# Filler products on TensorE: which planned gaps get them, in which bank, and how many

## The chip, the cores and the metric

The kernel runs on one core of one Trainium2 chip. The metric is device time in microseconds (us) of that core. Engine names are those of the profile: PE is TensorE's matmul, PEld its weight load, DVE is VectorE, ACT is ScalarE, POOL is GpSimd, SP is SyncE, which issues most transfers.

## The reference, cut to what matters

The reference is a chain of eight blocks on an activation `x` of 4 x 512 x 128 floats. Each takes the layer norm of x and adds its result back:

```python
x = x + L0_xcond(cond, ctx, _layernorm(x), ...)  # slot attention, 77 context rows, 3 iterations
x = x + L0_ffn(_layernorm(x), ...)               # routed experts, 8 of 128 -> 512 -> 128, top 2
x = x + L1_xcond(ctx, _layernorm(x), ...)        # attention, 16 heads of 64, over [ctx, x]
x = x + L1_ffn(_layernorm(x), ...)               # routed experts, top 1
x = x + L2_xcond(_layernorm(x), cond, ctx, ...)  # self attention, cross attention, gated ffn
x = x + L2_ffn(_layernorm(x), ...)               # 16 gated experts, top 2, and shared ones
x = x + L3_xcond(_layernorm(x), cond, ctx, ...)  # 6 layers: self and cross attention (16 heads of 8), ffn
x = x + L3_ffn(_layernorm(x), ...)               # router and ffn for half of the rows
```

None of this arithmetic is touched by the change. Filler products compute nothing that is used: `warm` multiplies the identity tile by itself (128 x 128 by 128 x 256, bf16) into a PSUM bank that the next real product overwrites.

## The kernel before

**Tiles and streams.** The four batch items stay in SBUF in `X`. Up to four streams of work run interleaved, in two sets of scratch tiles whose names begin with `c0` and `c1`. All products go to PSUM, which is cut into eight banks of 128 x 512 floats (four pairs). Every matmul in the profile therefore writes `ps`.

**The planner.** The order of work on each engine is fixed while the program is built. Each stream is a Python generator that yields wants: a chain of (engine, cost in us) steps, the buffers that it takes, and the time `after` which its data is ready. `Plan.merge` asks `Plan.ends` for the planned begin and end of each stream's next want, takes the one with the least key (its begin, with small weights), moves the planned clocks of the engines that the chain uses, takes the buffers and resumes the stream, which appends the step to `order` (`emit`). Each engine then walks this one list and issues its part of each step, in that order. Costs in the wants are hand-measured, `SLOW` scales them, `ORDER` holds the constants of each stage. Semaphores make the order safe; the plan's times have no force on the chip.

**Stages.** "0" is the slot attention (`stage0`, wants named `s0...`), "1" and "3" the routed experts (`routed`, products `re1` L1856 and `re2` L1866 behind `zbt` L1847), "2" and "4" the attentions with 64-wide heads (`attn64`: `mt` L1969, `sc` L1982, `av` L1998), "5" the gated experts, "6" the six layers (`attn6`: row maxima `m8` L2137, with DVE L2970 behind it, `m8t` L2159 and `m8w` L2168, scores `s8` L2179, `a8` L2193 and L2110 for the projections), and at the end of each stream `stage7`.

**Wants that matter here.** Most wants that use PE begin with it: `[("T", .6), ("A", .68)]` is a product and its eviction by ACT. Four begin on another engine and take a bank: `s0a` (DVE .35, then PE 1.3; L1755 and L1756, four times), `en` (DVE, POOL, DVE, then PE .2; L1808, once), `m8t` (DVE .42, PE .35; 48 times in stage 6) and `m8w` (DVE .5, PE .35; 24 times). Products that add to a bank which their stream already holds (`av`, `re2`, `a8` after the first) take no bank of their own.

**Filler before.** `Plan.idle` looks only at a want whose chain begins with PE and whose first buffer is a bank. The planned idle time is `w.after` less the later of PE's planned clock and the planned release of its buffers. If it is over 0.7, a `warm` step goes ahead of the want, into the want's own bank, with 0.6 of the idle time divided by 0.107 us products, at most 24. `warm` (L1714 to L1720) waits until the bank is free and issues its products without any other wait, so they start as soon as PE gets to them.

Of the kernel before, what the change touches and what calls it, by code (L numbers as in the profile page):

```python
# [31 lines left out]
    "6": dict(lag=0.0744, weight=0.0116, even=0.002, held=0.2624, table=1.1712, apart=55.6204, spread=0, seed=7961, stagger=13.3148, bias=dict(T=0.244, S=0.373, VTA=-0.191, TVb=-0.054, A=-0.534, VG=-0.949, G=-0.49, TA=-0.046, TAb=-0.043, TAV=0.203), turns=((13, 247, 0.3), (53, 150, 0.0), (379, 276, 0.3), (419, 456, 0.0), (3849, 853, 0), (3874, 138, 0.15), (3874, 642, 1.0), (4746, 100, 0), )),  # L32
}
PER_SEM = 8000
WARM_OVER, WARM_SHARE, WARM_MOST = 0.7, 0.6, 24
S128 = float(np.float32(128.0) ** np.float32(0.5))
S8 = float(np.float32(1.0) / np.float32(np.sqrt(np.float32(8.0))))

# [1 line left out]
class Sem:  # L40


    def __init__(self, nc, ctx, name, by=1):
        self.nc, self.ctx, self.name, self.by = nc, ctx, name, by
        self.n, self.tab, self.handles = 0, {}, []
# [56 lines left out]
class Bufs:  # L102
# [13 lines left out]
    def give(self, u, t=0.0):  # L116
        u.t = t
        self.free.append(u)
# [11 lines left out]
class Banks:  # L130
# [13 lines left out]
    def take(self):  # L144
# [6 lines left out]
        self.held[k] = True  # L151
        return u

    def give(self, u, t=0.0):
        u.t = t
        for k in u.at:
            self.use[k], self.held[k] = u, False
# [54 lines left out]
class Plan:  # L212


    def __init__(self):
        self.order, self.live, self.table = [], [], None
        self.clock = {"T": 0.0, "A": 0.0, "V": 0.0, "G": 0.0, "S": 0.0}

# [46 lines left out]
        self.would = table  # L265
        return (t if begin is None else begin) + self.held * held, r

    def idle(self, w):

        if not w.bufs or not isinstance(w.bufs[0], (Banks, Pairs, Last)):  # L270
            return 0.0
        ready = max(self.clock["T"], max(b.ready(w.bufs.count(b)) for b in w.bufs))
        return w.after - ready

    def merge(self, streams, owners=()):
        for s, o in zip(streams, list(owners) + [None] * len(streams)):
            self.spawn(s, o)
        idle = 0
        while self.live:
            idle += 1  # L280
            if idle > 6:
                raise RuntimeError("the streams wait for each other")
            best = None
            for x in list(self.live):
                if x[1] is None:
                    try:
                        x[1] = x[0].send(x[2])
                    except StopIteration:
                        self.live.remove(x)
                        idle = 0  # L290
                        continue
                    x[2] = None
                if x[1] is None:
                    continue
                e = self.ends(x[1])
                if e is None:
                    continue
                key = e[0] + (self.even * x[3].work if x[3] else 0.0) + self.weight * (e[1][-1][2] if e[1] else 0.0)
                key += self.bias.get(x[1].kind, 0.0)
                if self.spread:  # L300
                    key += self.spread * self.rng.rand()
                if best is None or key < best[0]:
                    best = (key, x, e[1], self.would)
            if best is None:
                continue
            idle = 0
            _, x, ends, self.table = best
            self.steps += 1
            idle_pe = self.idle(x[1]) if x[1].chain and x[1].chain[0][0] == "T" else 0.0
            if self.turns and self.steps >= self.turns[0][0]:  # L310
                _, seed, self.spread = self.turns.pop(0)
                self.rng = np.random.RandomState(seed)
            for eng, t, _ in ends:
                self.clock[eng] = t
            if x[3]:
                x[3].work += sum(step[1] for step in x[1].chain)
            x[2] = ([b.take() for b in x[1].bufs], [t for _, _, t in ends])
            if idle_pe > WARM_OVER:
                self.emit("warm", x[2][0][0], min(WARM_MOST, int(WARM_SHARE * idle_pe / 0.107)))
            x[1] = None  # L320


# [18 lines left out]
def build(nc, d, out):  # L341
    ctx = ExitStack()
    with ctx:
# [4 lines left out]
        T, A, V, G = (Sem(nc, ctx, n) for n in ("pe", "act", "dve", "pool"))  # L348
# [55 lines left out]
        banks = Banks(pairs)  # L404
# [3 lines left out]
        for i in range(2):  # L408
# [3 lines left out]
            n = f"c{i}"  # L412
# [18 lines left out]
            a, o = c.ar, 0  # L431
# [34 lines left out]
        for c in cos:  # L466
            a, o = c.ar, [9712]
# [157 lines left out]


        plan = Plan()
        emit, order = plan.emit, plan.order

        def ln_T(c, src, dst, t, scale=None, bias=None, by="V", dep=None):  # L630
# [2721 lines left out]
def program(nc, arrays):  # L3352
    d = {n: nc.dram_tensor("in_" + n, a.shape, mybir.dt.from_np(a.dtype), kind="ExternalInput").ap()
         for n, a in arrays.items()}
    out = nc.dram_tensor("out_0", (4, 512, 128), F32, kind="ExternalOutput").ap()
    build(nc, d, out)
# [13 lines left out]
```

## Time and profile before

| | |
|---|---|
| time, median of 3 runs | 3996.13 us (3988.41 to 3999.48) |
| the profiled execution | 4006.4 us |
| its span, first to last instruction | 4004.6 us |
| PE busy | 3550.0 us, 89% |
| DVE, ACT, POOL busy | 62%, 56%, 35% |
| mean granted TensorE clock | 0.962 of full speed |
| filler products recorded (L1720) | 1194 |

The profiled execution is 10.3 us above the median of the unprofiled runs. A granted clock of 1.0 is 2.4 GHz; the only other level in this trace is half of it. "The chain" is the chain of work that ended last, followed back from the last instruction.

### The profile page before, as it was taken

What the parts mean: (1) busy time and instruction counts of PE and PEld (TensorE: products, weight loads), DVE (VectorE), ACT (ScalarE), POOL (GpSimd) and SP (SyncE); (2) the same over time, 40 slices, a digit from 0 to 9 for tenths busy, and PEclk for the clock granted to TensorE, in tenths of its full rate; (3) what the DMA queues carried; (4) which work ended last, traced back from release to release, by engine and by line L of the source; (5) the groups of instructions that cost most, each with busy time, mean ns of one, the idle gap of its engine ahead of it and who ended that gap; (6) DMA issues with size and microseconds to landing.
All of it is one profiled execution on the core that took longest, in us unless ns stands there. A gap on an engine that the chain in (4) does not pass through costs nothing.

```text
span 4004.6 us, 59026 instructions
## 1 busy us (share of the span) xinstructions
PE 3550.0 (89%) x23055; PEld 1606.8 (40%) x23055; DVE 2497.9 (62%) x4786; ACT 2259.3 (56%) x3258; POOL 1421.1 (35%) x1419
## 2 busy tenths in 40 slices
PE   6778999999789999999987888999999989988987
PEld 5567333433733344334652232333333333333334
DVE  6743544544354346534659878777787778777755
ACT  4524554554245455545313767777777677677773
POOL 5543434334244303430013243443433433433322
PEclk7989999999899999999997999999999999999999
DMA  3021100000210010001111011110110110110100
GB/s 123 11 72 52 50 12 22 12 12 22 79 46 17 23 39 11 17 22 58 35 36 44 25 36 38 44 49 26 45 48 25 52 42 25 52 41 25 43 12 17
DMA packets 139224, 146.21 MB, mean 37 GB/s; under 512 B 37241, under 2 KB 120649, under 8 KB 137238
## 3 DMA queue, kind: packets, MB, share of 16 engines
q1 hardware_dynamic: 135876, 136.16, 11.6%
q0 software_dynamic: 3072, 6.30, 0.5%
q8 instruction: 183, 3.00, 0.3%
q14 instruction: 93, 0.76, 0.1%
HBM read 69.20 MB, written 12.59 MB: 20 GB/s over the span
## 4 chain that ended last, share of the span: by engine, by line
PE 57%; DVE 24%; ACT 9%; POOL 5%; issue 4%; DMA 1%; SPq 0%; POOLq 0%; DVEq 0%; ACTq 0%
PE ps L1998 6%; PE ps L1982 6%; PE ps L2193 5%; DVE c1sm L2970 4%; DVE c0sm L2970 4%; PE ps L2110 3%; PE ps L2179 3%; ACT wA L2442 2%; PE ps L2030 2%; PE ps L1923 2%; PE ps L2137 2%; PE ps L2237 2%; PE ps L2229 2%; PE ps L1866 2%; PE ps L1856 2%
## 5 line engine op out<-in xcount | busy, mean ns | idle before, releaser
L2442 ACT ACTIVATE wA<-ps 128x1024 f32<-128x1024 f32 (+1 forms) x576 | 580.8, 1023 | 192.5 <-PE ps L2179 188.0
L2970 DVE TENSOR_REDUCE c1sm<-ps 128x2 f32<-128x1024 f32 x384 | 454.8, 1220 | 103.7 <-PE ps L2137 102.1
L2970 DVE TENSOR_REDUCE c0sm<-ps 128x2 f32<-128x1024 f32 x384 | 453.4, 1220 | 95.1 <-PE ps L2137 93.8
L2745 DVE TENSOR_REDUCE c1sm<-ps 128x2 f32<-128x1024 f32 x128 | 154.4, 1222 | 186.8 <-PE ps L1947 184.8
L2745 DVE TENSOR_REDUCE c0sm<-ps 128x2 f32<-128x1024 f32 x128 | 154.7, 1222 | 164.7 <-PE ps L1947 157.2
L2442 ACT ACTIVATE c0m<-ps 128x1024 f32<-128x1024 f32 (+1 forms) x195 | 199.6, 1024 | 66.0 <-PE ps L2179 64.7
L2442 ACT ACTIVATE wB<-ps 128x1024 f32<-128x1024 f32 (+1 forms) x189 | 193.4, 1023 | 56.6 <-PE ps L2179 55.1
L3104 POOL TENSOR_SCALAR c1sm<-c1sm 128x4 f32<-128x4 f32 x40 | 7.8, 196 | 536.8 <-DVE c1sm L2514 536.7
L2179 PE MATMUL ps<-c0ar 64*128 64x512 bf16 (+1 forms) x864 | 166.5, 388 | 28.8 <-DVE c1sm L2970 12.0
L3104 POOL TENSOR_SCALAR c0sm<-c0sm 128x4 f32<-128x4 f32 x40 | 7.9, 196 | 512.0 <-DVE c0sm L2514 426.6
L1982 PE MATMUL ps<-c0ar 64*128 64x512 f32 (+1 forms) x640 | 177.7, 633 | 10.1 <-DVE c1sm L2745 4.0
L2193 PE MATMUL ps<-wA,c1m 128*9 128x512 f32 (+1 forms) x932 | 183.3, 603 | 1.5 <-ACT wB L2442 0.9
L2179 PE MATMUL ps<-c1ar 64*128 64x512 bf16 (+1 forms) x864 | 163.3, 386 | 22.1 <-DVE c0sm L2970 12.3
L3148 POOL TENSOR_TENSOR c0ar<-c0ar 128x1024 f32<-128x1024 f32 x52 | 122.9, 2363 | 159.6 <-ACT c0ar L2372 132.4
L1720 PE MATMUL ps<-CST 128*128 128x256 bf16 x1194 | 170.9, 297 | 8.7 <-DMA CST<-in_cst 7.9
L1982 PE MATMUL ps<-c1ar 64*128 64x512 f32 (+1 forms) x640 | 175.1, 624 | 3.6 <-DVE c0sm L2745 1.1
L2137 PE MATMUL ps<-c1ar 62*128 62x512 bf16 x768 | 151.5, 393 | 21.1 <-DVE c1sm L2970 6.9
L2372 ACT ACTIVATE c0ar<-ps 128x1024 f32<-128x1024 f32 (+1 forms) x96 | 98.3, 1024 | 119.3 <-PE ps L1985 118.8
L2137 PE MATMUL ps<-c0ar 62*128 62x512 bf16 x768 | 150.2, 391 | 17.3 <-DVE c0sm L2970 8.8
L3148 POOL TENSOR_TENSOR c1ar<-c1ar 128x1024 f32<-128x1024 f32 x49 | 116.9, 2385 | 134.7 <-ACT c1ar L2372 106.8
L3161 POOL TENSOR_TENSOR c0m<-c0m 128x512 f32<-128x512 f32 (+1 forms) x78 | 96.7, 1241 | 187.0 <-DVE c0m L2959 163.3
L2372 ACT ACTIVATE c1ar<-ps 128x1024 f32<-128x1024 f32 (+1 forms) x95 | 97.3, 1024 | 108.6 <-PE ps L1985 107.0
(981 smaller groups left out, 8409.9 us busy)
## 6 DMA issues: line engine op xcount, KB each, us to landing
c0ar<-c0m SPq DMA_DIRECT2D x216, 128.0 KB, 2.4
c1ar<-c0m SPq DMA_DIRECT2D x216, 128.0 KB, 2.4
c0m<-rscr SPq DMA_DIRECT2D x96, 128.0 KB, 3.0
c1m<-rscr SPq DMA_DIRECT2D x96, 128.0 KB, 2.9
wA<-in_x SPq DMA_DIRECT2D x1, 4112.0 KB, 21.9
wA<-in_x SPq DMA_DIRECT2D x1, 4096.0 KB, 12.7
wA<-in_lay SPq DMA_DIRECT2D x3, 1346.0 KB, 5.8
wB<-in_lay SPq DMA_DIRECT2D x3, 1346.0 KB, 5.6
```

The lines of the kernel that those rows point to most:

```text
L1720: e.matmul(u.ap[:, 0:256], one[:, 0:128], one, start=True, stop=True, skip_group_check=True)
L1982: e.matmul(j4(u.ap, h, 512)[0:n, :], c.KT[s][r, o:o + n], c.QT[s][r, :], start=True, stop=False)
L1998: x = e.matmul(acc.ap[64 - 64 * h:128 - 64 * h, :], c.VV[g % 2][0:n, i, 64 * h:64 * h + 64], P.ap[0:n, h, :], start=first, stop=end, skip_ ...
L2110: i = e.matmul(U.ap[:, 512 * k:512 * k + ncol], j4(ww, k), src, start=True, stop=True)
L2137: i = e.matmul(j4(u.ap, p, 512), c.QS[r, s, 128 * j:128 * j + 128], c.KS[r, s, :], start=True, stop=True)
L2179: i = e.matmul(j4(u.ap, p, 512)[0:n, :], K, c.QS[r, s, :], start=True, stop=True)
L2193: x = e.matmul(acc.ap[32 * i:32 * i + (9 if g % 2 else 18), :], vv, Ps[i // 2].ap[0:n, i % 2, :], start=first, stop=end, skip_group_check= ...
L2372: e.activation(P.ap[0:n, :, :], u.ap[0:n, :].rearrange("p (h q) -> p h q", h=2), ACT.Exp, scale=0.125).then_inc(*A(("P", n0, g, i), free=[u]))
L2442: e.activation(P.ap[0:n, :, :], u.ap[0:n, :].rearrange("p (a q) -> p a q", a=2), ACT.Exp, scale=S8).then_inc(*A(("P8", n0, s, k), free=[u]))
L2745: e.tensor_reduce(c.sm[:, 2 * (g % 2), 2 * j:2 * j + 2], u.ap.rearrange("p (h k) -> p h k", h=2)[:, :, 0:n], AX, ALU.max, negate=True).the ...
L2970: e.tensor_reduce(c.mneg[:, j, :, s // 4, s % 4], u.ap.rearrange("p (a k) -> p a k", a=2), AX, ALU.max, negate=True).then_inc(*V(free=[u]))
L3148: e.tensor_tensor(S.ap, P0.ap if P0 else S.ap, P.ap, ALU.add).then_inc(*G(("S", n0, g), free=[P0, P] if P0 else [P]))
```

## The change

`Plan.idle` goes; `Plan.fill` takes its place and is called for every chosen want. It finds the first PE step in the chain, wherever it stands, and its planned start. It keeps a list `pe` of PE's planned work, and sums what of it lies in the 3.4 us ahead of that start. It places filler if the planned gap ahead of PE's step is at least 0.5 us and the planned work in those 3.4 us is at most 0.85 of them. The bank is the want's own first bank, or, where it takes none, the free bank released earliest (`peek`, which takes nothing). The number is the least of 24, 0.8 of the room (from the later of PE's clock and the bank's release to the start), and what brings planned work to 0.95 of the 3.4 us. The order of all other steps stays what it was.

```diff
-WARM_OVER, WARM_SHARE, WARM_MOST = 0.7, 0.6, 24
+WARM_OVER, WARM_LOW, WARM_HIGH, WARM_SHARE, WARM_WINDOW, WARM_MOST = 0.5, 0.85, 0.95, 0.8, 3.4, 24
@@ class Banks
+    def peek(self):
+        k = min((k for k in range(len(self.aps)) if not self.held[k]), key=lambda k: self.use[k].t)
+        return Use(self.aps[k], [self.use[k]])
@@ class Plan
-    def idle(self, w):
-        if not w.bufs or not isinstance(w.bufs[0], (Banks, Pairs, Last)):
-            return 0.0
-        ready = max(self.clock["T"], max(b.ready(w.bufs.count(b)) for b in w.bufs))
-        return w.after - ready
+    def fill(self, w, ends, taken):
+        k = next((k for k, step in enumerate(w.chain) if step[0] == "T"), None)
+        if k is None:
+            return
+        now, start = self.clock["T"], ends[k][1] - w.chain[k][1]
+        self.pe = [x for x in self.pe if x[1] > start - WARM_WINDOW] + [(start, ends[k][1])]
+        busy = sum(b - max(a, start - WARM_WINDOW) for a, b in self.pe[:-1])
+        if start - now < WARM_OVER or busy > WARM_LOW * WARM_WINDOW:
+            return
+        bank = next((u for u, b in zip(taken, w.bufs) if isinstance(b, (Banks, Pairs, Last))), None)
+        if bank is None and self.banks.ready(1) is not None:
+            bank = self.banks.peek()
+        if bank is None:
+            return
+        room = start - max(now, max(p.t for p in bank.before))
+        n = min(WARM_MOST, int(min(WARM_SHARE * room, WARM_HIGH * WARM_WINDOW - busy) / 0.107))
+        if room > WARM_OVER and n > 0:
+            self.emit("warm", bank, n)
+            self.pe.insert(-1, (start - 0.107 * n, start))
@@ merge
-            idle_pe = self.idle(x[1]) if x[1].chain and x[1].chain[0][0] == "T" else 0.0
+            x[2] = ([b.take() for b in x[1].bufs], [t for _, _, t in ends])
+            self.fill(x[1], ends, x[2][0])
             for eng, t, _ in ends:
                 self.clock[eng] = t
-            x[2] = ([b.take() for b in x[1].bufs], [t for _, _, t in ends])
-            if idle_pe > WARM_OVER:
-                self.emit("warm", x[2][0][0], min(WARM_MOST, int(WARM_SHARE * idle_pe / 0.107)))
```

## Rows read from the trace of the kernel before

**Rows 1.** The page: granted clock in 40 slices; below it, the cores view.

```profile
PEclk7989999999899999999997999999999999999999
...
core 0: 4004.6 us, clock 0.962
```

**Rows 2.** Windows view: stretch, PE, PEld, DVE, ACT, POOL busy, granted clock, DMA.

```profile
17.00:54.50 37.50, 23.58 (x97) 19.58 (x98) 19.64 (x90) 13.85 (x33) 14.49 (x26) 0.50 0.34 135
...
75.00:85.00 10.00, 9.33 (x32) 7.05 (x33) 6.44 (x26) 4.32 (x9) 6.31 (x9) 0.50 0.06 26
300.00:2070.00 1770.00, 1626.23 (x9421) 793.73 (x9420) 847.23 (x1591) 826.43 (x1412) 559.29 (x320) 0.98 0.10 31
2070.00:2180.00 110.00, 71.47 (x334) 28.46 (x332) 90.82 (x160) 26.67 (x44) 44.51 (x56) 0.71 0.22 62
2180.00:3860.00 1680.00, 1521.76 (x11167) 549.43 (x11166) 1297.92 (x2017) 1211.61 (x1426) 634.36 (x755) 1.00 0.13 37
3860.00:4004.60 144.60, 110.85 (x758) 62.58 (x757) 75.91 (x223) 63.19 (x80) 31.95 (x36) 0.89 0.06 17
```

**Rows 3.** The chain over the whole span by engine; then the first 300 us by line.

```profile
PE 57%; DVE 24%; ACT 9%; POOL 5%; issue 4%; DMA 1%; SPq 0%; POOLq 0%; DVEq 0%; ACTq 0%
...
by line: issue 21.1%; PE ps L1856 5.2%; PE ps L1866 4.2%; ACT c0ar L2282 3.5%; PE ps L1720 3.2%; PE ps L1746 3.1%; PE ps L1778 3.0%; PE ps L1794 2.2%; POOL c0ar L3106 2.0%; DVE c0st L2510 1.8%; DMA X<-in_x 1.6%; ACT c1m L2282 1.6%; ACT c1ar
```

**Rows 4.** Source view of line L1720, filler: whole span, 0 to 300, stage 6.

```profile
L1720 PE MATMUL ps<-CST x1194: 269/273/421, 7.9 to 3987.3; 128*128 128x256 bf16 x199
...
L1720 PE MATMUL ps<-CST x545: 269/273/421, 7.9 to 268.2; 128*128 128x256 bf16 x182
...
L1720 PE MATMUL ps<-CST x23: 272/273/283, 2845.4 to 3439.7; 128*128 128x256 bf16 x23
```

**Rows 5.** PE's timeline: start, duration, line, and idle time before it.

```profile
7.86 5.30 PE L1720 MATMUL ps<-CST 128*128 128x256 bf16 x24 [7.86 <-DMA CST<-in_cst]
...
369.64 2.78 PE L1720 MATMUL ps<-CST 128*128 128x256 bf16 x24
381.08 1.12 PE L1911 MATMUL ps<-CST,c0m 128*128 128x128 f32 x4 [8.66 <-DVE c0m L2523]
```

**Rows 6.** The chain between 22 and 48 us, its PE pieces; then two at full clock.

```profile
22.24 0.68 PE ps L1755 x2
22.92 0.44 PE ps L1756 x2
...
38.78 1.12 PE ps L1746 x4
39.90 1.72 PE ps L1778 x2
...
105.78 0.66 PE ps L1746 x4
106.44 0.92 PE ps L1778 x2
```

**Rows 7.** The chain between 75 and 85 us, first and last of its six pieces.

```profile
75.67 0.27 PE ps L1808
...
82.96 1.72 PE ps L1801 x8
```

**Rows 8.** PE's waits from 2070 us on: total us, times, longest.

```profile
PE ps L2159 <- DVE c0sm L2986: 14.8, 19, 5.7
...
PE ps L2159 <- DVE c1sm L2986: 10.4, 20, 1.0
...
PE ps L2168 <- DVE c0sm L2995: 8.7, 12, 2.7
...
PE ps L2168 <- DVE c1sm L2995: 5.8, 11, 1.5
```

**Rows 9.** Windows view of the low-clock stretches in and behind stage 6.

```profile
2331.00:2334.40 3.40, 3.13 (x16) 0.39 (x8) 2.47 (x3) 1.78 (x3) 0.00 (x0) 0.50 0.06 19
...
2348.00:2355.00 7.00, 7.00 (x34) 1.21 (x26) 3.82 (x6) 2.65 (x3) 0.00 (x0) 0.51 0.00 0
```

More of the change, by code:

```diff
@@ L215, in __init__ @@
     def __init__(self):
+        self.pe, self.banks = [], None
         self.order, self.live, self.table = [], [], None
@@ L627, in build @@
         plan = Plan()
+        plan.banks = banks
         emit, order = plan.emit, plan.order
```

## The prediction, made before the changed kernel was run

> **What bounds the kernel now.** I read the clock first, because filler can pay in one way only: by keeping PE at its upper level. The slices and the mean over the core [rows 1] show a clock that is full almost everywhere: a mean of 0.962, where the lower level is 0.5, is (1 - 0.962) x 4004.6 / 0.5 = 304 us at the lower level. The windows view says where these lie [rows 2]. From 17 to 54.5 us the clock is low throughout, and from 75 to 85 us again; in the long middle, 300 to 2070 us, 0.98 leaves 0.02 x 1770 / 0.5 = 71 us; 2070 to 2180 us has 0.29 x 110 / 0.5 = 64 us, but there DVE is busy 83% of the time with row maxima and PE 65%; stage 6, 1680 us long, is at 1.00; the end, from 3860 us, has 0.11 x 144.6 / 0.5 = 32 us.
>
> The chain view says what a low clock costs [rows 3]: PE holds 57% of the chain, so a low clock is paid only where PE's real products are the chain. If the 304 us had PE on the chain in its mean share and all were brought to the upper level, the gain would be 304 x 0.57 / 2 = 87 us. That is the ceiling. The Trainium skill (TensorE: Matmul & The Clock Gate, Terms) puts the penalty at the throttled time x (1 - K/N), which here would be 304 x 0.5 = 152 us; the chain does not agree, since in the first low stretch only 9.1 of 37.5 us are PE's on it. The sum below goes by the chain.
>
> **What a filler product costs.** 24 of them take 2.78 us in the middle of the run and 5.30 us in the first group of the run, before PE has done anything [rows 5]: 2.78 / 24 = 0.116 with the last one's drain in it, so 0.11 us each, against about 0.22 us cold. The planner counts 0.107, so a cold group lasts twice what was planned. They sit in PE's queue ahead of a real step. If that step's data comes later than the group ends, they are free; if not, they are on the chain. In the first 300 us filler is 3.2% of the chain [rows 3], 9.6 us, out of 545 products [rows 4] x 0.11 = 60 us. So 16% of filler time is paid. I use this share for all filler. It makes 1194 x 0.11 x 0.16 = 21 us of filler on the chain today, over the span.
>
> **The change, part by part: costs.**
>
> (a) Share 0.6 to 0.8 and the threshold 0.7 to 0.5, at the steps that get filler already. The groups that are at the limit of 24 stay as they are; I counted 18 such groups in PE's timeline, of which [rows 5] has two, 430 of the 1194 products. The other 760 grow by a third: 250 products, 28 us of PE, x 0.16 = 4.4 us.
>
> (b) `m8t` and `m8w`, 72 steps in stage 6. The planner chooses such a want by the begin of its DVE part, and PE's part starts 0.42 or 0.5 us of DVE and a lag later, so planned gaps just about the new threshold of 0.5 are the rule unless PE's planned clock is ahead of DVE's. The real waits exist: lines L2159 and L2168 waited 66 times for 39.7 us in all [rows 8], 0.6 us each. In a 0.6 us gap behind dense work, 3.4 - 0.6 = 2.8 us are busy, and both limits give 4 products, 0.44 us. That is 72 x 4 = 288 products, 32 us. At 16% it would be 5 us; since 0.44 lies under the mean real wait, I take 3 us. Behind PE here are queued `m8`, `s8` and `a8` of the other streams, which feed DVE and ACT (77% and 72% busy [rows 2]), so a delay is passed on only in part. Bounds: 0 and 32 us.
>
> (c) `s0a` four times and `en` once, with up to 24 products each: at most 120 products, cold or warm 13 to 25 us; x 0.16 = 2 to 4, I take 2 us.
>
> (d) Products that take no bank (`re2`, `av`, `a8`). They wait for ACT's output, and PE in 300 to 2070 us is busy 92% [rows 2]: planned gaps of half a microsecond must be rare there. The trace does not show how many. Between none and 400 products, I take 100: 11 us, x 0.16 = 2 us.
>
> (e) The peeked bank, a new wait. `warm` waits for the release of the free bank that the plan frees first; a later step waits for the same bank or a younger one anyway. I cost it at nothing. If the plan is wrong by 0.2 us on 100 such steps, it is 20 us x 0.16 = 3 us. The limit of 0.95 and the ban over 0.85 take filler away where PE is dense; I count no gain for it, at most 2 us.
>
> Costs together: 4.4 + 3 + 2 + 2 = 11.4 us; 0 to (28 + 32 + 25 + 44) = 129 us if no or all filler is paid.
>
> **The change, part by part: gains.**
>
> (f) The opening. From 22 to 48 us the chain has six pieces of L1755 and L1756, two of L1746, two of L1778: 3.4 + 2.2 + 3.4 = 9.1 us at the low clock; at the high one L1746 takes 0.66 instead of 1.12, L1778 0.92 instead of 1.72 [rows 6], so 0.9 + 1.6 + about half of 3.4 = 4 us could come back. `s0a` comes just before, and gets filler for the first time. Its real gaps are longer than planned ones, so the clock may fall again: I take 3 us.
>
> (g) 75 to 85 us. The chain is PE for six pieces from 75.67 to 84.68 us [rows 7], 9.0 us, all cold, right behind the wait of `en`. Warm it would be about 4.5 us. I take 3.
>
> (h) Stage 6 and the end. Stage 6 has 10.4 us of low clock with PE busy in 10.1 of them [rows 9], the end 32 us with PE busy 77% [rows 2]. At half, 5 + 12 = 17 us of PE time, of which PE's share of the chain, 0.57, is 10 us. `m8w` and `m8t` steps stand ahead of some of these; I take 6. The 64 us before 2180 bring nothing: the maxima wait for banks that DVE frees, and `fill` allows no room before the bank's release.
>
> (i) Elsewhere. The falls of the clock in the middle follow long waits, such as 8.66 us behind a group that is already at 24 products [rows 5]. `fill` still puts one group at the head of the gap, at most 24 long, so the rest of such a gap stays empty. Of 71 x 0.57 / 2 = 20 us I take 1.5.
>
> Gains together: 3 + 3 + 6 + 1.5 = 13.5 us, between 0 and the ceiling of 87.
>
> **The sum.** 4006.4 - 13.5 + 11.4 = 4004.3 us for a profiled execution; less the 10.3 us by which it stands above the median of the runs, 3994 us. Gains and costs are small sums of many small things that nearly cancel.
>
> **The rivals.**
>
> Faster: the fuller rule keeps the clock up in the middle too. What speaks for it: many falls there follow mixed stretches in which short waits add up, and 0.8 for 0.6 with a lower threshold makes these stretches denser. What speaks against: PE is 92% busy there already. It would give half of (i), 10 us, all of (f) to (h), 4 + 4.5 + 10, less 4 of the costs saved: 28.5 - 7.4 = 21 us gained, 3975 us.
>
> Slower: filler ahead of `m8t`, `m8w` and bank-less products holds up PE in stage 6. The clock there is 1.00, so nothing can be bought. What speaks for it: 23 products in the whole stage today [rows 4], so nearly all would be new, and PE is 91% busy. It decides when more than half of 400 to 500 new products are paid: 450 x 0.11 x 0.6 = 30 us, less 13.5 of gain and with 8 of the other costs, 25 us lost, 4021 us. What speaks against: the real waits in front of just these steps. The Trainium skill (TensorE: Matmul & The Clock Gate, Part 3, "What overlaps and what doesn't") has matmuls in strict order, so nothing can pass a filler; the trace agrees with it, since the filler of the first 300 us does appear on the chain [rows 3].
>
> No effect: the planned gaps at the new places are mostly under 0.5 us or the 3.4 us ahead are over 0.85 full, so that few groups are added. Then only (a) is left, with about 1 us of gain: 3 us lost, 3999 us.
>
> **How the numbers follow.** Runs of the kernel before differ by 0.28%, so 0.3%, 12 us, is about what can be told from no change. Near balance, as in the sum: 0.34. No effect: 0.10. Faster rival or beyond: 0.32; slower rival or beyond: 0.24. Of the balanced case a tenth spills over the 12 us on the faster side. That gives faster 0.35, same 0.40, slower 0.25. The likeliest case alone is 3982 to 4006. The range for 8 in 10 must reach both outer rivals and somewhat past them, as their sizes are uncertain by half: 3962 to 4024.
>
> **What would show it.** In the profile after: L1720 with 1700 to 2100 products, of them 200 to 400 in stage 6; L2159 and L2168 with shorter waits and filler just before them; the clock of 17 to 54.5 us above 0.7, and of 75 to 85 us near 1.0; the mean clock at 0.967 to 0.975; filler's part of the chain in the first 300 us at 3.5 to 5%; 300 to 2070 us as long as before within 6 us. I am wrong if the mean clock passes 0.98 with the middle shorter (faster rival), if stage 6 grows by 15 us or more (slower), or if L1720 stays under 1400 (no effect).

## The result, and the profile after

The changed kernel takes 3999.99 us (median of 15 runs, 3997.54 to 4007.72) against 3992.03 us of the kernel before (15 runs): ratio 1.0021, 95% interval 1.0013 to 1.0029. It was repeated unchanged twice, as e5 and e12 below: 1.0006 (0.9997 to 1.0015) and 1.0019 (1.0010 to 1.0028). The mean of the three is 1.0015: it is slower by some 0.15%, 6 us, where a gain of 2 us was forecast. The time is inside the range, within the 0.3% that was called no change, and the sign is wrong.

The cores view and the source view of the filler line (L1738 in the changed kernel; all lines behind `Plan` moved by 18), for the whole span, for 0 to 300 us and for 2180 to 3860 us:

```profile
core 0: 4003.5 us, clock 0.968
...
L1738 PE MATMUL ps<-CST x1778: 269/273/422, 7.6 to 3984.6; 128*128 128x256 bf16 x198
...
L1738 PE MATMUL ps<-CST x775: 269/273/422, 7.6 to 265.7; 128*128 128x256 bf16 x194
...
L1738 PE MATMUL ps<-CST x118: 272/273/283, 2287.5 to 3814.8; 128*128 128x256 bf16 x118
```

Against [rows 4] there are 584 products more: 230 in the first 300 us, 95 in stage 6. The two orders, walked through side by side, say where: the 118 groups of before hold 248 products more, and 46 new groups hold 336. Of these, 4 groups (79) stand ahead of `s0a`, one (24) ahead of `en`, 20 (125) ahead of `m8t` and `m8w`, 3 (12) ahead of products without a bank; the other 18 (96) are ahead of steps that begin with PE.

The windows view of the changed kernel, for the stretches of [rows 2]:

```profile
17.00:54.50 37.50, 30.07 (x198) 24.17 (x196) 21.44 (x99) 13.79 (x33) 15.74 (x30) 0.81 0.34 136
75.00:85.00 10.00, 8.30 (x62) 6.53 (x61) 7.98 (x34) 5.79 (x12) 6.59 (x11) 1.00 0.06 26
300.00:2070.00 1770.00, 1645.64 (x9550) 807.22 (x9549) 846.24 (x1601) 823.71 (x1404) 558.94 (x320) 0.97 0.11 31
...
2180.00:3860.00 1680.00, 1534.01 (x11258) 559.25 (x11259) 1293.58 (x2012) 1208.64 (x1423) 632.30 (x754) 0.99 0.13 37
```

The opening's clock went from 0.50 to 0.81 and from 0.50 to 1.00. The middle's did not rise at all (0.98 in both traces of the kernel before, 0.97 in all three of the changed one), though PE is busy 19 us more there: that is filler that buys no clock.

The chain view by line, for the first 300 us of the changed kernel:

```profile
by line: issue 8.6%; PE ps L1738 7.2%; PE ps L1874 5.5%; PE ps L1884 4.3%; POOL zslots L3099 4.0%; DMA zslots<-c0ar 3.4%; ACT c0ar L2300 3.1%; PE ps L1764 3.0%; PE ps L1796 2.9%; ACT c1m L2300 2.6%; DVE c1st L2528 2.1%; PE ps L1865 1.8%; DV
```

Filler is 7.2% of the chain there, 21.6 us for 775 products, 25% of their 0.11 us each; it was 3.2% [rows 3], 16%. Summed over the chain of the whole span, filler holds 21 us before and 59 to 66 us in the three traces of the changed kernel. That is where filler lies, not yet what it costs: e8 below has 100 us of it there and is faster than both kernels.

PE's waits from 2070 us on, which answer to [rows 8]:

```profile
PE ps L2177 <- DVE c0sm L3004: 6.4, 15, 1.2
...
PE ps L2186 <- DVE c0sm L3013: 5.1, 12, 1.1
PE ps L2177 <- DVE c1sm L3004: 4.9, 14, 0.8
PE ps L2186 <- DVE c1sm L3013: 4.3, 9, 1.5
```

They fell from 39.7 to 20.7 us, the 5.7 us wait among them: filler fills real waits here. It did not make stage 6 shorter: from 2450 to 3860 us the changed kernel takes 1410.3 us, the two traces of before 1409.3 and 1410.1.

A caution on traces. The profiled execution of before in hand (4006.4 us) lies 14 us over the median of its 15 runs, so the two traces in hand are nearly equal in length (4004.6 and 4003.5 us). The totals below are ratios of timed runs, each to the kernel before on the same chip; from traces I take stretches, and say how far they repeat.

### The profile page after: what moved, and what is told of

It reads as the page before. It is cut to its first block, busy times and chain, and to the rows that moved or that the text cites. A ratio compares the mean times of both kernels' runs of the same rounds, so it can differ in the third digit from the quotient of the medians.

```text
span 4003.5 us, 60191 instructions
## 1 busy us (share of the span) xinstructions
PE 3601.8 (90%) x23639; PEld 1650.3 (41%) x23639; DVE 2494.8 (62%) x4786; ACT 2256.7 (56%) x3258; POOL 1418.0 (35%) x1419
## 4 chain that ended last, share of the span: by engine, by line
PE 59%; DVE 23%; ACT 8%; POOL 5%; issue 3%; DMA 1%; SPq 1%; DVEq 0%; POOLq 0%; ACTq 0%
PE ps L2016 7%; PE ps L2000 7%; PE ps L2211 5%; DVE c0sm L2988 4%; DVE c1sm L2988 3%; PE ps L2128 3%; PE ps L2197 3%; ACT wA L2460 2%; PE ps L1941 2%; PE ps L2048 2%; PE ps L2155 2%; PE ps L2255 2%; PE ps L2247 2%; PE ps L1874 2%; PE ps L1884 2%
## 5 line engine op out<-in xcount | busy, mean ns | idle before, releaser
L2460 ACT ACTIVATE wA<-ps 128x1024 f32<-128x1024 f32 (+1 forms) x576 | 580.0, 1022 | 190.8 <-PE ps L2197 186.1
L2763 DVE TENSOR_REDUCE c0sm<-ps 128x2 f32<-128x1024 f32 x128 | 154.7, 1221 | 169.3 <-PE ps L1965 167.0
L1738 PE MATMUL ps<-CST 128*128 128x256 bf16 x1778 | 244.7, 291 | 9.4 <-DMA CST<-in_cst 7.6
L1738 PEld LDWEIGHTS ps<-CST 128*128 128x128 bf16 x1778 | 180.4, 105 | 69.2 <-issue 27.5
## 6 DMA issues: line engine op xcount, KB each, us to landing
wA<-in_x SPq DMA_DIRECT2D x1, 4112.0 KB, 21.6
```

The lines of the kernel that those rows point to most:

```text
L1738: e.matmul(u.ap[:, 0:256], one[:, 0:128], one, start=True, stop=True, skip_group_check=True)
L2460: e.activation(P.ap[0:n, :, :], u.ap[0:n, :].rearrange("p (a q) -> p a q", a=2), ACT.Exp, scale=S8).then_inc(*A(("P8", n0, s, k), free=[u]))
L2763: e.tensor_reduce(c.sm[:, 2 * (g % 2), 2 * j:2 * j + 2], u.ap.rearrange("p (h k) -> p h k", h=2)[:, :, 0:n], AX, ALU.max, negate=True).the ...
```

## The experiments

Lengths named "the stretch" are between the same two DVE instructions in each trace; both kernels have the same 5068 of them (semaphore steps, drains and memsets left out) in the same order. Times such as 1885 to 2075 us name these instructions by where they lie in the trace of the kernel before.

**e1, the kernel before again.**

> The kernel before, unchanged, as a control: what a repeat shows and what its usual trace looks like. Its profiled execution in hand (4006.4 us, mean clock 0.962) lies 14 us above the median of its 15 runs (3992 us), so the two traces in hand differ by less than the two kernels do. Both theories: ratio 1.000, within 0.001. Mean clocks of the runs between 0.960 and 0.968. If the usual clock is near 0.968, as in the changed kernel's runs, the change buys no clock at all.

Measured: 1.0006 (0.9997 to 1.0015). Clocks of its runs 0.961 to 0.964, in the trace 0.963. So the change does raise the clock (to about 0.970), and 0.1% is as fine as these runs resolve.

**e2, the old places with the new numbers; e3, the new places beside the old numbers.** The method `idle` is put back, and `old` is its value for the want.

```diff
 # e2, in fill
+        if old <= 0.7:
+            return
         if start - now < WARM_OVER or busy > WARM_LOW * WARM_WINDOW:
             return
 # e3, in fill
+        if old > 0.7:
+            n = min(WARM_MOST, int(0.6 * old / 0.107))
+            self.emit("warm", taken[0], n)
+            self.pe.insert(-1, (start - 0.107 * n, start))
+            return
```

> The new number of products (1442 for 1194), but only at the 118 places that the old rule chooses. Theory length: the added products at the old places are paid more often than the 16% of my sum, since the first 60% of a planned gap were the safe ones: 248 x 0.11 = 27 us of PE, a third to a half of it on the chain, so 1.002 to 1.003 here, as in the full change. Theory places: this part is harmless, 1.000 to 1.001, and the loss sits in the 46 new groups. Computation unchanged.

> The old number at the old places, and the 46 new groups with 336 products beside them (1530 in all). Theory places: most of the loss is here, 1.002 to 1.003, stage 6 longer by 5 us or more. Theory length: no loss here, and the opening's gain shows: 0.998 to 1.000. Computation unchanged.

Measured: e2 1.0007 (0.9998 to 1.0016), median clock 0.965; e3 0.9996 (0.9986 to 1.0007), clock 0.971. Neither shows a loss of its own in the total; the new places bring most of the clock. In the gated experts' stage the two differ: the stretch from 1885 to 2075 us takes 191.0 us in e2 and 194.2 in e3 (189.2 and 189.0 in the two traces of before), though e3 adds only 20 products there, in four new groups, and e2 32. The theory that the new places hold up stage 6 is not borne out: from 2450 to 3860 us e3 takes 1408.9 us, the two traces of before 1409.3 and 1410.1.

**e4, the opening's five groups alone.** e3 with the condition `w.kind in ("VTV", "VGVTV")` for new groups.

> The kernel before with five new groups only: ahead of the four steps that begin with DVE in the opening (L1755 in the trace before) and of the one ahead of L1808, 103 products, 1297 in all. By my terms (f) and (g) less (c) it gains 4 us; the two traces in hand show up to 5 us gained by 124 us. Theory length and theory places both: 0.998 to 0.9995. If it is 1.000 or above, what is gained in the opening is given back before the end of the first stage, behind the scatter that POOL issues from 231 us on.

Measured: 0.9998 (0.9989 to 1.0007), median clock 0.967. At most 4 us of gain, and none that is clear. Its trace takes 131.5 us from 0 to 138 us, the two of before 132.0 and 132.2.

**e5, the changed kernel again.**

> The changed kernel, unchanged, beside the kernel before on one chip. Its recorded ratio was 1.0021 (1.0013 to 1.0029). Its two halves, each alone, gave 1.0007 (old places, new numbers) and 0.9996 (new places, old numbers), which add to 1.0003, and a repeat of the kernel before gave 1.0006 (0.9997 to 1.0015) against itself. Theory interaction: the two halves together cost more than their sum (a longer group ahead of a step plus a new one behind it), then 1.002 again. Theory small: the change is worth nothing that is stable, 0.9995 to 1.001 here, and much of the recorded 0.2% belongs to the runs and not to the kernel.

Measured: 1.0006 (0.9997 to 1.0015), clock 0.970.

**e6, the new groups of stage 6 and the end alone.** e3 with the condition `self.name == "6"`.

> The kernel before with the new groups of stage 6 and the end only: 26 groups, 170 products, 1364 in all. Theory places: 1.0010 to 1.0025. Theory length or theory small: 0.9995 to 1.0007, since these steps wait for DVE anyway.

Measured: 0.9994 (0.9985 to 1.0003). No loss: the theory of places falls here too.

**e7, no filler at all.**

```diff
-            self.emit("warm", bank, n)
```

> The changed kernel with every filler product left out (the real computation stays whole). It sizes what filler buys at all. If filler matters at the 118 old places, the clock's mean falls to 0.93 or below and the ratio is 1.005 to 1.015. If filler is nearly balanced by its own time on the chain everywhere, 0.998 to 1.003, and then it is no surprise that 584 more products change nothing.

Measured: 1.0042 (1.0029 to 1.0056), 5 runs, median clock 0.943. Without any filler (the real work is all there) the kernel loses 0.42%, 17 us, against the one with 1194 products. The clock's fall from 0.964 to 0.943 is 0.021 x 4004 / 0.5 = 168 us more at the lower level, and that count is too low: the granted clock reads 1.00 from 7 to 54.5 us in e7, while L1746's sets of four transposes (L1763 there) take 1.06 to 1.12 us each in that stretch, as at the lower level [rows 6]. All filler together is worth 17 us, so a further half of it had little to win.

**e8, long groups.**

```diff
         n = min(WARM_MOST, int(min(WARM_SHARE * room, WARM_HIGH * WARM_WINDOW - busy) / 0.107))
+        if room > WARM_WINDOW:
+            n = min(96, int(WARM_SHARE * room / 0.107))
```

> The changed kernel, but in planned gaps over 3.4 us the group covers 0.8 of the gap up to 96 products, where the change stops at 24: 2567 products in all. My step (i) says that the falls of the clock in the middle come behind such gaps and stay because a group is at most 24 long. Then the mean clock rises to 0.978 or more and the time falls by 5 to 12 us against the changed kernel: 0.998 to 0.9995. If real gaps are often shorter than planned ones, the groups are on the chain, most of all in the opening, and it is 1.001 to 1.004.

Measured: 0.9988 (0.9979 to 0.9997), median clock 0.982, against 1.0006 for e5 on the same chip. 789 more products, and faster than both kernels. Filler is 17.1% of the chain of its first 300 us, against 7.2% in the changed kernel, yet the first 206 us take 192.5 us, against 195.8 to 197.2. What decides is where a product stands, not how many there are, and time of filler on the chain is a loss only where it brings back no clock.

**e9, e10, e13: the gated experts' stage.** Here PE has hardly any idle time. PE's timeline of the changed kernel, from 1922 us:

```profile
1922.30 1.88 PE L2090 MATMUL ps<-c0m,wB 128*128 128x512 f32 x4
1924.02 1.02 PE L2096 MATMUL ps<-c0m,wA 128*128 128x512 f32 x2
1924.88 0.82 PE L1738 MATMUL ps<-CST 128*128 128x256 bf16 x6
1925.53 1.02 PE L2056 MATMUL ps<-c1m,wA 128*128 128x512 f32 x2
...
1930.68 0.60 PE L1738 MATMUL ps<-CST 128*128 128x256 bf16 x4
1931.12 1.02 PE L2056 MATMUL ps<-c1m,wA 128*128 128x512 f32 x2
```

And the same place in e1:

```profile
1922.52 1.88 PE L2072 MATMUL ps<-c0m,wB 128*128 128x512 f32 x4
1924.24 1.02 PE L2078 MATMUL ps<-c0m,wA 128*128 128x512 f32 x2
1925.10 1.02 PE L2038 MATMUL ps<-c1m,wA 128*128 128x512 f32 x2
```

Read the starts: each product begins before the one ahead of it has drained, and no row has an idle time in brackets. Between L2096 and L2056 at 1924 us there was 0.86 us from start to start; now there is 1.51. The group of 6, and that of 4 at 1930.68, were placed because the plan had a gap there that the chip has not. The 0.65 us between them are 0.11 us for each of the 6: a filler product costs its full time here.

> The changed kernel with no filler in the gated experts' stage (about 1885 to 2075 us of the trace): 15 groups and 159 products fewer. Theory paid: what the change added sits mostly where PE has no idle time, so it is on the chain nearly in full, not at the 16% of my sum. Filler on the chain in this stretch is 2.8 us before and 12.7 us after the change. Then the stretch from 1885 to 2075 us falls from 194.4 us to 187 to 190 us (before the change 189.0), and the time by 4 to 7 us: ratio 0.9990 to 1.0000. Theory clock: without this filler the clock falls there and the stretch stays at 192 us or more; ratio 1.0005 to 1.002.

> The changed kernel with twice the number of products in every group of the gated experts' stage; 1925 products in all, 147 more. It measures the price of a filler product at the margin. Theory paid: 0.07 to 0.11 us each, the stretch from 1885 to 2075 us is longer by 10 to 16 us, ratio 1.003 to 1.005. Average theory (16% of 0.11 us): longer by 2.6 us, ratio 1.0005 to 1.002.

> The changed kernel with the old places and numbers in the gated experts' stage only (52 products fewer, 1726 in all). Theory margin: there is a best amount. The old 107 products hold the clock there, the added 52 stand where PE has no idle time and are paid in full. Then the stretch from 1885 to 2075 us returns from 194.4 us to 189 to 191 us (with none it was 194.0, with twice as many 202.7), and the ratio to the kernel before is 0.9990 to 1.0005 instead of about 1.0015. If the stretch stays at 194 us, the loss there comes from what is changed ahead of it.

```diff
 # e9, in fill
-        if room > WARM_OVER and n > 0:
+        if room > WARM_OVER and n > 0 and self.name != "5":
 # e10, below the same line
+            if self.name == "5":
+                n *= 2
 # e13, in fill; e14 is the same with "12345"
+        if self.name in "5":
+            if old > 0.7:
+                self.emit("warm", taken[0], min(WARM_MOST, int(0.6 * old / 0.107)))
+            return
```

The source view gives a length for the stage, from the start of the first gate product on c0m to that of the last on c1ar (rows of e1; the changed kernel; e9; e10; e13; and of e7, which has no filler anywhere):

```profile
L2072 PE MATMUL ps<-c0m,wB x36: 592/592/595, 1903.1 to 1950.0; 128*128 128x512 f32 x36
...
L2072 PE MATMUL ps<-c1ar,wB x36: 592/592/697, 2028.6 to 2056.8; 128*128 128x512 f32 x36
```

```profile
L2090 PE MATMUL ps<-c0m,wB x36: 592/592/595, 1902.2 to 1950.9; 128*128 128x512 f32 x36
...
L2090 PE MATMUL ps<-c1ar,wB x36: 592/592/697, 2032.3 to 2060.6; 128*128 128x512 f32 x36
```

```profile
L2091 PE MATMUL ps<-c0m,wB x36: 592/592/1061, 1899.4 to 1945.2; 128*128 128x512 f32 x36
...
L2091 PE MATMUL ps<-c1ar,wB x36: 592/592/697, 2028.1 to 2056.3; 128*128 128x512 f32 x36
```

```profile
L2093 PE MATMUL ps<-c0m,wB x36: 592/592/595, 1899.3 to 1952.0; 128*128 128x512 f32 x36
...
L2093 PE MATMUL ps<-c1ar,wB x36: 592/592/697, 2037.9 to 2066.1; 128*128 128x512 f32 x36
```

```profile
L2103 PE MATMUL ps<-c0m,wB x36: 592/593/596, 1898.5 to 1945.4; 128*128 128x512 f32 x36
...
L2103 PE MATMUL ps<-c1ar,wB x36: 592/592/697, 2025.4 to 2053.7; 128*128 128x512 f32 x36
```

```profile
L2089 PE MATMUL ps<-c0m,wB x36: 592/592/595, 1910.8 to 1955.8; 128*128 128x512 f32 x36
...
L2089 PE MATMUL ps<-c1ar,wB x36: 592/592/697, 2037.2 to 2065.5; 128*128 128x512 f32 x36
```

| | filler products of the stage | of these within the length | length, us | whole kernel to before |
|---|---|---|---|---|
| kernel before (e1) | 107 | 62 | 153.7 | |
| changed kernel | 159 | 101 | 158.4 | 1.0019 (e12, same chip as e9, e10) |
| e9, none here | 0 | 0 | 156.9 | 0.9994 (0.9984 to 1.0004) |
| e7, none anywhere | 0 | 0 | 154.7 | 1.0042 (1.0029 to 1.0056) |
| e10, double | 306 | 202 | 166.8 | 1.0026 (1.0016 to 1.0037) |
| e13, old ones | 107 | 62 | 155.2 | 1.0002 (0.9993 to 1.0010) |

For the DVE stretch from 1885 to 2075 us it is 189.0 (e1), 194.5 (changed), 194.0 (e9), 190.1 (e7), 202.7 (e10) and 190.8 us (e13). How far these lengths repeat, the other traces tell. The three traces of the changed kernel have 158.4 us each. With the 62 old products the length is 153.8 us in the first trace of before too, but 155.2 to 155.7 in e4, e6, e13, e14 and e15: in the traces of before, one place without any filler of its own takes 3.1 us, in these five 4.3 to 4.8. So against e13 the 39 added products cost 3.2 us, 0.08 us each; against e1 it is 4.7 us, of which some 1.5 are this place, which is slower in the changed kernel as well. From 101 to 202 products the length grows by 8.4 us, 0.08 us each again. Both are about three quarters of a product's 0.11 us.

With none it is 156.9 us in e9, where I had expected a gain, but 154.7 in e7 and 154.6 in e11 (below), so a best amount is not shown: none and the old number are within the spread of each other. What sets e9's trace apart is the clock at the head of the stage, mostly ahead of this length. Its value is the third from the right in the windows view of e9, then of the changed kernel, then of e7:

```profile
1880.00:1901.00 21.00, 10.95 (x42) 7.46 (x43) 12.03 (x52) 3.71 (x6) 0.00 (x0) 0.51 0.12 28
```

```profile
1880.00:1901.00 21.00, 15.04 (x100) 9.93 (x101) 12.80 (x58) 5.86 (x9) 1.20 (x2) 0.85 0.09 28
```

```profile
1880.00:1901.00 21.00, 15.08 (x112) 9.14 (x108) 10.32 (x42) 6.66 (x14) 1.20 (x2) 0.90 0.09 27
```

That the missing filler let it fall is not shown, since e7 has none either and stands at 0.90.

What remains unexplained: e9's stage is only 1.5 us shorter than the changed kernel's, but its timed runs are 0.25%, 10 us, faster than e12's. Its trace has a few us less behind the stage, at 2180 to 2450 us (270.9 for 273.4), a place that also differs between two executions of one kernel (below). That this is the cause was not shown.

**e11 and e15, long groups and less of the rest; e12, the changed kernel a third time.** e11: as e8, with the old numbers at most at the old places, new groups only of kinds `VTV`, `VGVTV` and stage 6's `VTA`, and no short group in the gated experts' stage. e15 puts these short groups back, with the old numbers.

> What the runs so far point to: filler only where gaps are real. Long groups (0.8 of planned gaps over 3.4 us, up to 96 products) as in the earlier run at 0.9988, the opening's new groups, the old numbers at the old places otherwise, none in short gaps of the gated experts' stage: 2115 products. Theory paid: 3 to 6 us better than the long groups alone, 0.9970 to 0.9985, with a mean clock of 0.980 or more. If the small added groups cost nothing it stays at 0.9988.

> The changed kernel once more beside the kernel before. The recorded ratio is 1.0021 (1.0013 to 1.0029), the first repeat 1.0006 (0.9997 to 1.0015). Theory small: 1.0005 to 1.002 again, so that the change costs 2 to 8 us; both intervals would then hold their part of one value near 1.0013.

> The lean kernel with long groups (0.9979), with the old short groups of the gated experts' stage put back (2198 products). There the long groups alone gave 190.0 us for the stretch. Theory margin: with the old short groups back it is 189 to 191 us and the whole 0.9975 to 0.9990, no clear difference to the lean one: filler pays where real gaps are long and is near balance everywhere else.

Measured: e11 0.9979 (0.9968 to 0.9990), median clock 0.979; e12 1.0019 (1.0010 to 1.0028), clock 0.970; e15 0.9974 (0.9963 to 0.9985), 7 runs, the gated experts' stretch at 190.0 us in e11 and 189.5 in e15. These two are the fastest, 0.21% and 0.26% under the kernel before, at 2115 and 2198 products. Their intervals overlap: the 83 short-group products between them make no clear difference.

**e14, the change only in the opening and from stage 6 on.**

> Old places and numbers in all stages from the first routed experts to the gated experts (1612 products); the change stays in the opening and from stage 6 on. Theory margin: the loss of the change is in this middle (206 to 2075 us), and what is left is its better half: 0.9980 to 0.9995. If it stays at 1.001 or above, the loss is in the opening or in stage 6 and my reading of the stretches is wrong.

Measured: 0.9984 (0.9974 to 0.9993), 1612 products; the gated experts' stretch is 191.1 us. By the timed runs this puts the loss in the middle: leave that as it was, and the change gains 0.16%, 6 us. Against the mean of the changed kernel's three ratios, 1.0015, e14 gives back 0.31%, 12 us, for 166 products fewer, and e13, which restores the gated experts' stage alone, 0.13%, 5 us, for 52 fewer (its trace: 3.7 us in the DVE stretch).

Where in the middle the other 7 us lie is not shown. From 206 to 2075 us the traces of the changed kernel take 1871.3, 1868.0 and 1867.3 us, that of e14 1863.9, but that of e13 1864.0 and the two of before 1868.4 and 1861.9: two executions of one kernel differ here by more than the effect. And e14's trace is of the slowest of its 12 runs, 12 us above their median.

## Why the prediction was wrong, point by point

**The step that failed** is the price in (a) and (d): "I use this share for all filler", the 16% of filler time that lay on the chain before, put on the added products too. The number was forecast well: 250 more products at the old places (248 measured), 1700 to 2100 in all (1778). The price was not. e14 against the changed kernel sizes it for the middle: 12 us for 166 products, 0.07 us each net of any gain, two thirds of the 0.11 us, where I had 16%. The gated experts' stage has it in the traces: 0.08 us a product, three quarters, and the full 0.11 where a group stands between two products that follow each other without a gap. Why the mean did not carry over: 16% is a mean over what was there; the added products are the last of each group, or stand where the plan's gap was the smallest, and in this stage such places have no idle time on PE. For the rest of the middle that reason is argued and not shown. A further case is in the routing stage, behind 206 us. PE's timeline of e1, then of the changed kernel:

```profile
212.33 4.33 PE L1720 MATMUL ps<-CST 128*128 128x256 bf16 x23
216.49 0.60 PE L1746 MATMUL ps<-CST,c0ar 128*128 128x128 f32 x4
```

```profile
207.26 5.08 PE L1738 MATMUL ps<-CST 128*128 128x256 bf16 x24
212.17 0.60 PE L1764 MATMUL ps<-CST,c0ar 128*128 128x128 f32 x4
```

and DVE's wait for PE behind each of them:

```profile
218.88 0.19 DVE L2663 TENSOR_SCALAR c0ar<-ps 128x32 f32<-128x32 f32 x1 [1.12 <-PE ps L1815]
```

```profile
214.56 0.19 DVE L2681 TENSOR_SCALAR c0ar<-ps 128x32 f32<-128x32 f32 x1 [2.33 <-PE ps L1833]
```

A group planned at 24 x 0.107 = 2.6 us ran for 5.1 us, 0.21 us a product, at a granted clock of 0.51 (207 to 212 us), and DVE waited 1.2 us longer. With 23 products here DVE waits 1.1 us in five traces (before, e1, e3, e4, e6) and 1.85 in e14; in the three of the changed kernel it waits 2.0 to 2.3. The stretch from 206 to 262 us is 62.0 to 62.9 us in the three traces of the changed kernel, 60.8 to 61.6 in five with the old numbers there, but also 62.3 in e14, which has them too: about 1 us, and not clear of the spread. I had named this ("a cold group lasts twice what was planned") and not priced it.

**Sizes of the parts.** By e14 the opening and stage 6 together gain 6 us; my (f), (g), (h) less (b), (c) made 7. These steps hold as a sum. In the opening alone, 0 to 138 us, three traces of the changed kernel take 127.3, 128.7 and 128.3 us, three with the old opening 132.0, 132.2 and 128.7: about 3 us of my 6 less 2. But the five new groups alone (e4) have 131.5 and no filler at all (e7) 130.8, so which groups bring it is open. The middle (206 to 2075 us) was to cost 4.4 + 2 less 1.5, about 5 us; e14 against the changed kernel says 12 us.

**(b)**, 72 groups with 288 products, was 20 groups with 125: the planned gap is often under the threshold, and stage 6 is as long as before. **(d)**, 100 products, was 12. Both were set too high in number, which hid part of the error in price. **(e)**, the peeked bank: only 3 groups use it, too few for its cost to show. **(i)** was right in kind: groups that stop at 24 leave the falls behind long gaps, and e8 brings 0.18% against the changed kernel by lengthening them. Its trace is shorter than those of the changed kernel by 3 to 5 us up to 206 us, and by 5 to 8 from 374 to 1885 us.

**Two readings.** The waits of [rows 8] are 62 and not 66, which changes nothing in (b). And the 10.3 us that the sum takes off for the profiled execution rest on 3 runs; by the 15 runs it is 14.4 us, and the same sum gives 3990 us, with the same gain of 2 us over the median.

**What was to show it.** L1738 with 1778 products, the mean clock at 0.968 and the two low stretches at 0.81 and 1.00 came as forecast. Stage 6 has 118 products instead of 200 to 400, and filler on the chain of the first 300 us is 7.2% instead of 3.5 to 5%: that was a sign of the wrong price, though e8 shows that such time can pay for itself.

**Rivals.** The slower rival had the right sign and the wrong place: I put the loss in stage 6, where clock 1.00 left nothing to buy. By that very argument it should have been the middle, also at 0.98. The price of a low clock was about right, if anything too high: at least 168 us more at the lower level (e7) cost 17 us plus the filler time saved. I estimate that time by filler's 21 us on the chain before, which makes 17 + 21 = 38 us, at most 0.23 us for each. Half of PE's share of the chain is 0.57 / 2 = 0.29. The Trainium skill's penalty of one half per us (TensorE: Matmul & The Clock Gate, Terms) would make it 84 us; the measurement does not agree.

**Not settled:** where 7 of the 12 us of the middle lie (above), and the halves: e2 and e3 add to 1.0003, the whole gives 1.0006 to 1.0021. Whether the two halves together cost more than their sum, or this is the 0.1% that the intervals leave, stays open.

## What to carry to other kernels

Price an added amount by the place of its last unit, not by the mean of what is there: work that is free in a real gap is paid in full in a gap that exists only in the plan, as the 6 products at 1924 us were. Filler pays ahead of long waits that the trace confirms, sized to the wait; in stretches where the timeline shows no idle time it should be left as it is or removed. Look also at whether a higher mean clock came with a shorter span: here 0.964 to 0.970 came with a longer one.

## What the runs showed of the hardware that was not expected

Executions of one kernel differ in steps. The stretch from 2180 to 2450 us took 273.0 us in one trace of the kernel before and 269.1 us in the other, with some 10 us [rows 9] and none at the lower clock; 262 to 374 us took 106.5 and 103.6, and 98.8 in e6, whose order there is that of the kernel before. Laid side by side product by product, the two traces of the kernel before part or meet by 0.6 to 2.3 us at some two dozen places; between them, as from 2450 to 3860 us, they repeat (1409.3 and 1410.1 us). So the trace of before in hand lies 14 us over the median of its kernel and that of e14 12 us, and the difference of two single traces says nothing about 0.2%.

At the head of a trace the granted clock can read 1.00 while PE works at its lower level. In the kernel before, the first 24 filler products take 5.30 us, 0.22 each, in a stretch that reads 1.00 (7 to 13 us); in e7 the first 54.5 us read 1.00 while each set of four transposes in them takes 1.06 to 1.12 us, against 0.66 at the upper level. There the durations tell the clock, and the reading does not.
